# VectorE scales the first 128 columns of a head's probabilities, GpSimd the other 256, in the attention ahead of the expert units

## The reference, cut to what matters

```
q = (x @ Wq).reshape(b, t, h, e).transpose(0, 2, 1, 3)      # 8 heads of 128 channels
...
dot = jnp.einsum('bhqe,bhke->bhqk', q, k)
dot = jnp.where(causal[None, None], dot, -jnp.inf)
att = jax.nn.softmax(dot, axis=-1)
out = jnp.einsum('bhqk,bhke->bhqe', att, v)
return out.transpose(0, 2, 1, 3).reshape(b, t, h * e) @ Wo + bo
```

## Time and profile before

| | us |
|---|---|
| median of 3 runs | 2448.54 (2445.33 to 2454.02) |
| the profiled execution's own time | 2440.3 |
| its span in the profile | 2438.6 |
| stage of the first 256 heads (826 to 1472 us of the span) | 646 |
| stage of the other 256 heads, with expert units (1472 to 2320 us) | 848 |

### The profile page before, as it was taken

One profiled execution on the slowest core, in us unless ns is written; L12 is line 12 of the kernel. 1 busy time (PEld: TensorE's weight loads), 2 busy tenths in 40 slices (PEclk: granted clock), 3 DMA queues, 4 the chain that ended last, 5 costly groups with the idle time before them and its releaser, 6 DMA issues.

```text
span 2438.6 us, 57785 instructions
## 1 busy us (share of the span) xinstructions
PE 2205.6 (90%) x16248; PEld 1922.4 (79%) x16248; DVE 1678.9 (69%) x8172; ACT 1647.4 (68%) x5185; POOL 1504.7 (62%) x1821
## 2 busy tenths in 40 slices
PE   4999978677777699999999999999999999999977
PEld 3888856344445588888888889999999999999965
DVE  4888767666554476777767676777768878778733
ACT  3878845122222577777777778888888888888854
POOL 6545100476777478888888885544544677547554
PEclk9999989899999899999999999999999999999999
DMA  2676689244444341121212116666664888568587
GB/s 77 211 241 229 232 203 138 80 142 138 139 141 140 111 98 55 38 56 38 55 38 55 38 51 192 174 170 178 176 168 122 247 246 253 159 191 249 165 257 242
DMA packets 357902, 361.87 MB, mean 148 GB/s; under 512 B 35604, under 2 KB 301693, under 8 KB 357585
## 3 DMA queue, kind: packets, MB, share of 16 engines
q1 hardware_dynamic: 321376, 272.95, 40.8%
q0 software_dynamic: 33472, 78.98, 9.8%
q10 hardware_dynamic: 2736, 6.25, 0.8%
HBM read 208.38 MB, written 144.00 MB: 145 GB/s over the span
## 4 chain that ended last, share of the span: by engine, by line
PE 63%; DVE 12%; POOL 10%; issue 6%; DMA 4%; ACT 2%; SPq 2%; ACTq 0%; DVEq 0%; POOLq 0%
PE bank L2297 7%; PE bank L2215 6%; PE bank L2203 6%; PE bank L2226 5%; PE bank L2261 4%; PE bank L2269 4%; PE bank L2242 3%; PE bank L2243 3%; PE bank L2241 3%; PE bank L2212 3%; POOL table L927 2%; DMA rows<-table,idx 2%; PE bank L2002 2%; POOL pr_place L979 2%; PE bank L2174 2%
## 5 line engine op out<-in xcount | busy, mean ns | idle before, releaser
L956 POOL DMA_INDIRECT zbuf<-pc,kb x248 | 249.9, 1008 | 166.1 <-DVE pc L1876 117.1
L1171 ACT ACTIVATE pr_place<-pr_place,nmax 128x128 f32<-128x128 f32 x512 | 205.5, 401 | 162.8 <-DVE nmax L1663 160.1
L950 POOL DMA_INDIRECT spread_rows<-kb,pos x248 | 252.7, 1019 | 99.2 <-issue 46.3
L1661 DVE CUSTOM_DVE_ANT_0 pr_place<-bank,causal 128x128 f32<-128x128 f32 x512 | 145.9, 285 | 207.6 <-PE bank L2215 203.7
L2226 PE MATMUL bank<-ident,pr_place 128*128 128x128 f32 x1536 | 254.2, 274 | 15.4 <-POOL pr_place L979 14.4
L1173 ACT ACTIVATE pr_place<-pr_place,nmax 128x256 f32<-128x256 f32 x512 | 254.7, 497 | 0.0
L1180 ACT ACTIVATE pr_place<-bank 128x384 f32<-128x384 f32 x512 | 251.0, 490 | 2.5 <-PE bank L2226 0.9
L2203 PE MATMUL bank<-x_part,wqk_part 128*128 128x256 f32 x1536 | 246.2, 296 | 2.1 <-DVE g_part L1683 1.1
L979 POOL TENSOR_SCALAR pr_place<-pr_place,rinv 128x256 f32<-128x256 f32 x256 | 245.2, 958 | 0.0
L2297 PE MATMUL bank<-wvo_part,x_part 128*128 128x512 f32 x768 | 231.5, 410 | 1.4 <-ACT vo_place L1257 1.4
L918 POOL DMA_INDIRECT rows<-table,idx x128 | 126.4, 987 | 151.4 <-DVE idx L1575 113.0
(11 more groups left out here) (361 smaller groups left out, 6251.0 us busy)
## 6 DMA issues: line engine op xcount, KB each, us to landing
pa<-bundle SPq DMA_DIRECT2D x196, 321.0 KB
table<-rows SPq DMA_DIRECT2D x96, 576.0 KB
rows<-table SPq DMA_DIRECT2D x192, 128.0 KB
wu_more<-bundle SPq DMA_DIRECT2D x65, 321.0 KB
kb<-spread_rows SPq DMA_DIRECT2D x248, 65.0 KB
junk<-zbuf SPq DMA_DIRECT2D x31, 512.0 KB
h3buf<-wqk SPq DMA_DIRECT2D x64, 128.0 KB
kb<-kb SPq DMA_DIRECT2D x31, 256.0 KB, 3.3
```

The lines of the kernel that those rows point to most:

```text
L950: pool.indirect_dma_start(out=spread_rows, out_offset=bass.IndirectOffsetOnAxis(ap=pos[:, k, j:j + 1], axis=0), in_=xr4s[g % 2][:, k, j], ...
L956: pool.indirect_dma_start(out=zbuf, out_offset=bass.IndirectOffsetOnAxis(ap=xu_at(t)[:, C + 1:XW].bitcast(U32), axis=0), in_=yu[:, t % YR] ...
```

## The change

POOL's `normalise` keeps the 256 columns and loses the 128. DVE runs `norm_first` for all 512 heads, not only for the last 256; for the first 256 it raises `pr_ready` with it. PE's `turns` now waits, for the first 256 heads, for both POOL's and DVE's semaphore. Nothing changes for heads 256 to 511.

```diff
             def normalise(u, h):
                 pool.wait_ge(rinv_ready, u + 1)
-                pool.tensor_scalar(pr[:, u % PRN, 0:P], pr[:, u % PRN, 0:P], rinv[:, h % 4, 0:1], None, ALU.mult)
                 pool.tensor_scalar(pr[:, u % PRN, P:3 * P], pr[:, u % PRN, P:3 * P], rinv[:, h % 4, 1:2], None, ALU.mult)\
                     .then_inc(pr_ready_pool, 1)
...
             def norm_first(u, h):
                 dve.wait_ge(rinv_ready, u + 1)
-                dve.tensor_scalar(pr[:, u % PRN, 0:P], pr[:, u % PRN, 0:P], rinv[:, h % 4, 0:1], None, ALU.mult)
+                ins = dve.tensor_scalar(pr[:, u % PRN, 0:P], pr[:, u % PRN, 0:P], rinv[:, h % 4, 0:1], None, ALU.mult)
+                if u < POOL_NORM:
+                    ins.then_inc(pr_ready, 1)
...
                             low(4 * n + h // 2)
-                        if there(u - N_LAG) and u - N_LAG >= POOL_NORM:
+                        if there(u - N_LAG):
                             norm_first(u - N_LAG, (h - N_LAG) % H1)
...
             def turns(u, h):
                 if u < POOL_NORM:
                     pe.wait_ge(pr_ready_pool, u + 1)
-                else:
-                    pe.wait_ge(pr_ready, u + 1 - POOL_NORM)
+                pe.wait_ge(pr_ready, u + 1)
```

## The result

The changed kernel takes 2439.99 us (median of 8 runs, 2435.87 to 2443.41), the kernel before 2452.15 us beside it (8 runs, 2445.33 to 2460.33): a ratio of 0.9947, with a 95% interval of 0.9932 to 0.9962. That is 13 us, or 0.53%, less, and clear of noise. Measured again beside four other kernels, it was 0.9939 (0.9922 to 0.9956). The forecast was 5 us less, within what can't be told from no change. In all that follows one execution, of the kernel with eight slots, ran at a granted clock of 0.74 and took 2835.86 us; it is left out of the ratios.

A forecast was written before the change was run, and what follows sets the result against it. PE was taken as the bound, busy 621.5 of 646 us. 0.18 + 0.25 = 0.43 us less per iteration, times 14 = 6, less about 1, gave 5 us: 2443.5 from 2448.5; range from two us below 2433.5 to 2461.

The forecast's parts named there:

- The path: Per iteration: DVE delays PE from slot 12, POOL's waits return in 5 to 7, the earlier root helps to slot 9.
- What POOL loses: POOL saves 0.61 us a head; PE's waits for it in slots 5 to 7 go, worth 1.05 us an iteration.
- The price of one addition: DVE's time for each added scaling of 128 columns: 0.20 us in even slots, 0.30 in odd ones.
- the high end: Highest price of an added DVE instruction: 0.42 us, from L1710's 500 ns less 0.08 of overlap; 13 us more in all.
- the third rival: DVE stands still until POOL's instruction is done, price 0.7 us in slots 13 and 5: 2454 us; chance 0.08.
- Slots 12 to 14: Three DVE additions cost 0.70 us, the cast gives 0.23 back: PE's scores of the next slot 0 come 0.47 later.
- Slot 0 and 1: The addition in slot 0 delays DVE's maxima of slot 1; half a step, 0.10 us, was counted.
- Slots 5 to 8: DVE 0.55 late, plus 0.30, less 0.19 and 0.30: maxima 0.36 late; 0.54 spare, so PE reaches slot 8 0.18 early.
- Slots 7 to 9: POOL's earlier root ends DVE's 1.16 us wait; at the gates' rows PE gets 0.25 us back.
- the first rival: DVE's additions are covered or paid for; PE gets 1.05 us back in 14 iterations, 15 us: 2433.5 us; chance 0.22.
- The second rival: DVE becomes the bound, slower, at a price of 0.32 us or more on the same path: 2457.5 us; chance 0.22.
- The signs that I had named: If right: no POOL or root waits, maxima waits some 0.5 us in slots 14 and 0, addition near 0.33, stage 641 us.

The follow-up runs named there:

- eight slots: Changed kernel, with DVE scaling the first 128 columns only in slots 1 to 4, 6 and 9 to 11, POOL in the others: 0.9901, 2431.68 us.
- nobody scales: Changed kernel without the added DVE instruction, so the first 128 columns of the first 256 heads stay unscaled: 0.9906, 2432.65 us.
- POOL filled: Changed kernel, with POOL still running a 128-column scaling, constant tile to scratch tile, for each of the first 256 heads: 1.0000, 2454.56 us.
- other eight: Changed kernel, with DVE scaling the first 128 columns only in slots 0, 5, 7, 8 and 12 to 15: 0.9981, 2449.32 us.
- root later: Changed kernel, with POOL's inverse root for the gates in slot 7 instead of 6, in the later stage as well: 1.0049, 2466.07 us.

## Why the prediction was right in its path and wrong in its size

The table is worked out from the traces. For each run it gives the shift against the kernel before, in us, at five places of an iteration, averaged over iterations 2 to 13 and counted from the transposes of slot 12. The last column is the change of the whole iteration; a minus is time saved.

| | scores slot 0 | scores slot 4 | maxima slot 6 | scores slot 8 | scores slot 10 |
|---|---|---|---|---|---|
| prediction | +0.47 | +0.55 | +0.36 | -0.18 | -0.43 |
| changed kernel | +0.16 | +0.29 | +0.04 | -0.48 | -0.84 |
| nobody scales | -0.23 | -0.23 | -0.66 | -1.18 | -1.56 |
| POOL filled | +0.39 | +0.51 | +0.45 | +0.24 | +0.18 |
| eight slots | -0.15 | -0.12 | -0.54 | -1.06 | -1.43 |
| other eight | +0.22 | +0.32 | +0.42 | -0.10 | -0.27 |
| root later | +0.17 | +0.29 | +0.03 | -0.49 | +0.11 |

**The path.** Each step is there with its sign: DVE pays in slots 12 to 1, PE gets POOL's waits back in 5 to 7 but not in full because the maxima of slot 6 come no earlier, and slots 7 to 9 give something more by the root. The run with the root one slot later is the same as the changed kernel up to slot 8 and then loses 0.95 us, which shows the last step by itself.

**What POOL loses** (0.61 us a head, PE's waits worth 1.05 us): right. PE waits for POOL nowhere, with POOL filled the gain is gone, and where nobody scales, PE gets 0.95 us back between slots 4 and 8 (from -0.23 to -1.18).

**The price of one addition**, 0.20 in even slots and 0.30 in odd ones: the second was too high. From the start of the added instruction to the next one it took 0.19 us in slots 12, 14 and 0, 0.20 in slot 13 and 0.21 in slot 5 (means over iterations 2 to 13). L1710's 500 ns, from which the high end was taken, don't carry over: this operation takes two scalars for each partition where the added one takes one, and 390 ns even now; the reason why POOL stretched it is below, at the third rival.

**Slots 12 to 14**, 0.70 less 0.23: this is the step that was mis-sized. Measured is +0.16 instead of +0.47, and that makes 0.31 of the 0.41 us by which an iteration came out better. The three additions took 0.58 and not 0.70, and 0.42 came back instead of 0.23: 0.27 at the cast, and 0.16 at the two instructions behind it (L1739 and L1744), which I had left out. POOL's shorter work alone gives 0.23 back here (the run in which nobody scales); that this is the number I had for the cast is luck, since there the cast gives 0.17. The rest comes by the addition itself: in that run the cast still ran beside POOL's scaling, 260 ns in the mean, and behind the added instruction it takes 166. So the addition pushes its follower out of POOL's way and pays a half of its own price.

**Slot 0 and 1**, 0.10: measured 0.13, right.

**Slots 5 to 8**, 0.30 - 0.19 - 0.30, and 0.54 spare: the maxima of slot 6 moved 0.25 earlier against PE's scores of slot 4, where I had 0.19, and the scores of slot 8 another 0.52. Right.

**Slots 7 to 9**, 0.25 back from the gates' rows: 0.36 came back.

**The sum**: 0.84 us, times 14, is 11.8 us; forecast were 0.43 and 6. The first two iterations cost 0.2 us (from DVE's first inverse to the transposes of slot 12 in iteration 1, 57.4 us instead of 57.2), where I took 1. That the forecast of 2443.5 us is only 3.5 above the measured median is luck in part: it started from 2448.54, the median of three runs, and that of eight is 2452.15. The gain itself is more than twice the 5 us that were forecast.

**The rivals.** The size is near that of the first rival (15 us), its mechanism isn't: it wanted PE's waits for DVE no longer than before, and they are, 5.6 us at the scores and 7.3 us of a new one. Nor is DVE's addition covered: without it another 10 us go. The second rival, slower, would have needed a price of 0.32 in the five slots; even with POOL filled it is 0.19 to 0.22 in slots 12, 13, 14 and 0, and 0.31 in slot 5. The mean of 0.354 us in that run comes from other slots.

The third was that DVE stands still while POOL works. As it was priced, to the end of POOL's instruction, it didn't happen. But the reading that I set against it, that the two engines only slow each other (0.39 us for each L1710), went by a mean of four and hides what happens. From each of the four at 1198.22 to DVE's next start it was 0.34, 0.26, 0.45 and 0.26 us, and 0.25 in the changed kernel where POOL was idle beside it: two of the four weren't slowed. The added instruction shows the pattern. In the eight profiled runs that have it, what it took depended on how long POOL's 256-column scaling (0.93 us) had been running when DVE's instruction started:

| started after, us | how many | what they took |
|---|---|---|
| 0.05 to 0.27 | 116 | 114 ended 0.54 to 0.58 us behind POOL's start, whenever they had begun: 0.29 to 0.49 us |
| 0.30 to 0.48 | 473 | all 0.27 to 0.29 us |
| 0.48 to 0.74 | 40 | 38 ended 1.00 to 1.03 us behind POOL's start, most of them 0.08 behind its end: 0.30 to 0.52 us |
| 0.74 and more | 141 | all 0.28 to 0.29 us |

So DVE does stand still, in two stretches of POOL's instruction, and goes on undisturbed between them. In slots 13 and 15 of the changed kernel the added instruction started 0.34 to 0.44 us into the scaling, in the free part, and cost 0.20 us; the one at 1204.98 started 0.24 into it and took 0.31. I had not foreseen this, and by the table it would have cost more had POOL started 0.2 us later.

The rule of the Trainium skill from which the rival came (SBUF — State Buffer, "Who interferes with whom") says that the second blocks for the whole instruction of the first. These rows agree that one engine stands still, and don't agree that it is for the whole instruction. That the added instruction runs in a two-port mode isn't shown directly; 128 columns more cost it 0.07 us (0.28 and 0.35 us), where they cost the maxima 0.13 (0.29 and 0.42 us).

**The signs that I had named.** No wait for POOL, no wait of L1711 for the root, and a later stage as before: these came. The wait for the maxima grew to 5.6 us, 0.4 in each iteration, where I had 0.5 in each of two slots; the added instruction took 0.290 us and not 0.33; and the stage is 12 us shorter and not 5.

**Its chances.** "Within 0.3%" had the most (0.45), and the result is 0.53% faster, which had 0.30. The range held the time. The prices were too cautious in one direction: for the odd slots and for the high end I went by L1710, a different instruction, rather than by the 0.28 us of the same one in the later stage.

## What to carry to other kernels

Where a hand-written pipeline has two engines that are late at different places, moving work between them should be decided slot by slot: eight instructions of an iteration were worth 24 us where the giver was late and the taker idle, and 5 us in the other slots. Look ahead of the whole chain for whoever waits on the relieved engine for something else: here a root of four columns, queued behind the scalings, cost 14 us when it came one slot later. And two waits in one period need not add up in full, since the time lost at the first is slack for the engine behind the second. When an instruction looks slowed beside another engine, list its single durations with the start of the other's instruction before taking a mean: here the mean of four hid two that weren't slowed.

## What the runs showed of the hardware that was not expected

- What a DVE instruction loses beside POOL hangs on the moment at which it starts within POOL's instruction, as the table at the third rival shows: the same scaling of 128 x 128 took 0.28 us when it started 0.30 to 0.48 us into POOL's 256-column scaling, and up to 0.49 us when it started 0.05 to 0.27 us into it.
- The cast of 128 x 8 takes 414 ns in the mean in the kernel before and 166 in the changed one. Before, it started 0.11 to 0.17 us into a scaling of POOL's in 13 of 15 iterations; now it starts 0.87 us or more into one, at its end. The row L1702 (128 x 4, 398 ns, now 170) ended 0.03 us ahead of the end of a scatter's issue in 13 of 15.
- A POOL memset, which reads nothing, held up the added instruction, too: 12 of them started 0.12 to 0.14 us into one and ended 0.08 us behind its end, after 0.50 us.
